# An expert layer that computes every expert, or only each token's two chosen ones

## The reference, cut to what matters

```
flat   = tokens                                  # (2048, 64)
probs  = softmax(flat @ router_w.T)              # 8 experts
p, idx = top_k(probs, 2);  p = p / (sum(p) + 1e-9)
gates  = p scattered to the 8 experts            # (2048, 8), six of the eight are zero
h1 = einsum('nc,ehc->neh', flat, w1)             # e = 8, h = 682
h3 = einsum('nc,ehc->neh', flat, w3)
h  = silu(h1) * h3
y  = einsum('neh,ech->nec', h, w2)               # back to 64 channels
out = einsum('ne,nec->nc', gates, y)
```

## Time and profile before

| | us |
|---|---|
| median of three runs (lowest, highest) | 957.54 (954.67, 958.70) |
| span of the profiled execution, first to last instruction | 952.8 |
| PE busy, PE weight load, DVE, ACT, POOL | 800.3, 594.2, 570.5, 556.2, 366.6 |
| mean granted TensorE clock (1 is full) | 0.741 |

### The profile page before, as it was taken

The page is one execution under the profiler, slowest core; times in us unless marked ns, Lnnn a source line. Parts: engine busy times, 40 slices in busy tenths (PEclk is TensorE's granted clock), DMA queues, the critical chain, the costliest instruction groups (busy, mean ns, idle before and its releaser), DMA issues.

```text
span 952.8 us, 18695 instructions
## 1 busy us (share of the span) xinstructions
PE 800.3 (84%) x6356; PEld 594.2 (62%) x6356; DVE 570.5 (60%) x1752; ACT 556.2 (58%) x1664; POOL 366.6 (38%) x297
## 2 busy tenths in 40 slices
PE   5899987777777776789988768999689999899995
PEld 3587875555655555566666547889446666466663
DVE  3888854556456466334344346887457667467765
ACT  3676752333355365334444355777478888588884
POOL 0878620000000000003000007874268888588884
PEclk7999995555555555555555556999689999899998
DMA  9700000000001100000000000000000100200001
GB/s 224 175 2 1 2 1 1 1 1 1 0 1 78 78 1 1 1 0 1 1 1 1 1 1 1 2 1 2 1 1 2 59 21 2 80 1 2 2 1 23
DMA packets 5860, 18.54 MB, mean 19 GB/s; under 512 B 1093, under 2 KB 2822, under 8 KB 5254
## 3 DMA queue, kind: packets, MB, share of 16 engines
q1 hardware_dynamic: 5478, 17.21, 6.2%
q10 hardware_dynamic: 288, 0.13, 0.1%
HBM read 9.47 MB, written 0.52 MB: 10 GB/s over the span
## 4 chain that ended last, share of the span: by engine, by line
PE 41%; POOL 22%; DVE 13%; issue 11%; ACT 11%; DVEq 1%; POOLq 1%; DMA 0%; SPq 0%; ACTq 0%
POOL zw L1007 21%; PE bank L558 10%; PE bank L383 6%; PE bank L560 6%; PE bank L400 6%; DVE bank L1320 5%; PE bank L348 4%; DVE hr L1324 4%; ACT bank L885 4%; ACT bank L889 4%; PE bank L524 2%; PE bank L370 1%; DVE hid L1089 1%; PE bank L315 1%; PE bank L413 1%
## 5 line engine op out<-in xcount | busy, mean ns | idle before, releaser
L1007 POOL TENSOR_TENSOR zw<-hid,zw 128x512 f16<-128x512 f32 x176 | 203.9, 1159 | 49.3 <-ACT zw L928 38.9
L558 PE MATMUL bank<-hr,lv 64*64 64x8 f32 x512 | 97.0, 261 | 98.8 <-DVE hr L1324 98.4
L966 POOL TENSOR_TENSOR st<-tent,tentx 128x768 f32<-128x768 f32 x72 | 112.2, 1589 | 173.3 <-DVE tentx L1081 123.8
L1443 DVE SCALAR_TENSOR_TENSOR hid<-bank,wsc,st 128x512 f32<-128x512 f32 x176 | 131.9, 750 | 76.0 <-ACT st L932 70.1
L558 PEld LDWEIGHTS bank<-hr,lv 64*64 64x64 f32 x512 | 72.8, 201 | 158.4 <-DVE hr L1324 158.2
L885 ACT ACTIVATE bank<-bank 64x16 f32<-64x16 f32 x256 | 39.2, 153 | 196.8 <-PE bank L560 196.5
L604 PE MATMUL bank<-st,wh 128*128 128x512 f16 x352 | 136.9, 389 | 11.5 <-POOL st L1000 5.4
L932 ACT ACTIVATE st<-bank,wsc 128x512 f32<-128x512 f32 x176 | 120.9, 687 | 39.8 <-PE bank L605 22.0
L605 PE MATMUL bank<-st,wl 128*128 128x512 f16 x352 | 136.8, 389 | 0.0
L966 POOL TENSOR_TENSOR st<-sq 128x768 f32<-128x768 f32 x9 | 13.2, 1498 | 309.3 <-DVE sq L1309 308.5
L1320 DVE TENSOR_TENSOR_SCAN bank<-bank,scan_add 64x24 f32<-64x24 f32 x256 | 52.9, 207 | 127.8 <-ACT bank L885 127.5
(11 more groups left out here) (184 smaller groups left out, 1340.4 us busy)
## 6 DMA issues: line engine op xcount, KB each, us to landing
w13s<-w SPq DMA_DIRECT2D x8, 704.0 KB, 17.9
w2f<-w SPq DMA_DIRECT2D x4, 384.0 KB, 25.4
w13s<-wh SPq DMA_DIRECT2D x2, 704.0 KB, 3.7
w13s<-wl SPq DMA_DIRECT2D x2, 704.0 KB, 5.0
wh<-w13s SPq DMA_DIRECT2D x2, 704.0 KB, 3.9
wl<-w13s SPq DMA_DIRECT2D x2, 704.0 KB, 5.1
w2f<-w2p SPq DMA_DIRECT2D x2, 384.0 KB, 4.9
w2p<-w2f SPq DMA_DIRECT2D x2, 384.0 KB, 5.7
```

What stands on the lines that cost most here:

```text
L558: nc.tensor.matmul(both[:, 0, t, :], lv[:, C:2 * C], prev, start=False, stop=True, skip_group_check=True)
L966: nc.gpsimd.tensor_tensor(st[p][:, t, k:k + KG, :].rearrange("p k (y x) -> p k y x", x=16), ty, tx, ALU.mult)\
L1007: nc.gpsimd.tensor_tensor(hl[:, u % MR, :], hid[:, u % MR, :], hh[:, u % MR, :], ALU.subtract)\
L1443: nc.vector.scalar_tensor_tensor(out=hid[:, u % MR, :], in0=bank[2 + u % 2][:, :], scalar=wsc[:, 5:6], in1=silu[:, u % 2, :], op0=ALU.mult ...
```

## The change

Only the two chosen experts of a token are computed. The 4096 (token, choice) entries are sorted by expert on the chip, each expert's list is padded to whole tiles of 128 entries, and NT = 39 tiles (the most that 4096 entries and 8 experts can need) are always run. The parts:

1. Weights. Each pair's weights lie as two slots of w1 and w3 side by side (2 x 682 columns) instead of padded blocks of 128; 16 pieces a pair are split, in 68 steps of the recurrence, to where they stay. SP's copies are gone; the loads are 52 DMAs instead of 12.
2. POOL makes constants (iotas, a triangle of ones, a float16 identity) between the convolutions.
3. After the logits, PE transposes `xn` to rows of tokens, ACT and POOL split them into high and low float16 parts, and SP writes them to DRAM (`xrows`, 2048 rows of 256 bytes).
4. DVE finds both choices from the logits, counts ranks by a scan, gets totals from two small PE matmuls, and so the place of every entry in the sorted order. 32 one-hot matrices (`lsel`, `tsel`) and 32 PE matmuls invert that order into row numbers (`xidx` for reading, `yidx` for writing), and a table `etab` says which expert a tile has.
5. Per tile: POOL gathers 128 rows of `xrows` (`fetch`, an indirect DMA, four ahead); SP copies that expert's second-layer weights (196 KB) to one of three buffers `w2r` (a register read from `etab` gives the address); PE turns the tokens, runs eight matmuls of 341 columns with the weights as moving operand, turns the hidden values (six float32 transposes) and runs twelve matmuls of 128 columns; ACT, DVE as before but 682 columns wide, and DVE also makes the low part; POOL scatters 128 rows of the result to DRAM (`spread`, an indirect DMA).
6. At the end SP reads the two results of every token back (1 MB), and DVE multiplies by the gates and adds.

There is no hardware loop any more; all 39 tiles are written out. The core of the diff:

```diff
# SP
+            for t in range(NT):
+                e = sp.value_load(etab[0:1, t:t + 1], min_val=0, max_val=E - 1)
+                if t >= 3:
+                    sp.wait_ge(s("m_y"), t - 2)
+                sp.dma_start(w2r[:, t % 3, :], w216[:, bass.ds(e * HP + 2 * HP, HP)])\
+                    .then_inc(s("m_w2" + "abc"[t % 3]), 16)
+            sp.wait_ge(s("m_rows"), 16 * NT)
+            for q in range(2):
+                sp.dma_start(ytok[:, 8 * q:8 * q + 8, :, :] ..., rows[:, q * 1024:q * 1024 + 1024])
# PE
+            for j in range(8):
+                mm = nc.tensor.transpose(bank[4 + j // 4][...], xn[:, j * 128:j * 128 + 128], ident[:, :])
...
+            def turn_tokens(t):
+                pe.wait_ge(s(f"m_g{t % AHEAD}"), 16 * (t // AHEAD + 1))
...
+                nc.tensor.transpose(bank[4][:, 0:64].bitcast(F16), xg[:, t, :], ident16[:, :])
+            def first(t, e):
+                pe.wait_ge(s("m_xts"), t + 1)
+                for m in range(2):
+                    if t > 0:
+                        pe.wait_ge(s(("m_silu", "m_hid")[m]), t)
+                    for half in range(2):
+                        for part in range(2):
+                            mm = nc.tensor.matmul(duo[m][:, half * 512:half * 512 + n], xts[:, t % 3, :],
+                                                  w16[:, bass.ds(e * SLOT + at, n)], ...)      # n = 341
+            def turn_hidden(t):
+                pe.wait_ge(s("m_hid"), t + 1)
+                for b in range(EB):                                                            # EB = 6
+                    mm = nc.tensor.transpose(bank[6 + b // 4][...], htok[:, t % 2, b * 128:...], ident[:, :])
+            def second(t):
+                pe.wait_ge(s("m_w2" + "abc"[t % 3]), 16 * (t // 3 + 1))
...
+                for b in range(EB):
+                    for part in (hh, hl):
+                        mm = nc.tensor.matmul(bank[5][:, 0:2 * C], part[...], w2r[...], ...)
+            for t in range(NT + 2):
+                if t < NT:
+                    first(t, e)
+                    if t + 1 < NT:
+                        e = expert(t + 1)              # value_load on PE
+                        turn_tokens(t + 1)
+                if 1 <= t <= NT:
+                    turn_hidden(t - 1)
+                if t >= 2:
+                    second(t - 2)
# ACT, per tile: gated(t) silu 682 columns; turned_tokens(t + 1) copy of 128; high(t - 1) copies of 512 and 256
# DVE
+            for c in range(32):
+                ins = nc.vector.tensor_scalar(lsel[:, c, :], lane_c[:, :], lane[:, k, g:g + 1], code_v[:, c:c + 1],
+                                              ALU.is_equal, ALU.mult)
...
+            for t in range(NT + 2):
+                if t < NT:
+                    gated(t)                           # 682 columns
+                if 1 <= t <= NT:
+                    low(t - 1)                         # 512 and 256 columns from PSUM
+                if t >= 2:
+                    rows_out(t - 2)                    # reduce_sum 128 -> 64 columns
# POOL
+            for t in range(AHEAD):                     # AHEAD = 4
+                fetch(t)
+            gp.wait_ge(s("m_idx"), 2)
+            for t in range(NT):
+                if t + AHEAD < NT:
+                    fetch(t + AHEAD)                   # waits for turn_tokens(t), then indirect DMA
+                spread(t)                              # waits for rows_out(t), then indirect DMA
```

More of the change, by code:

```diff
@@ new lines, in build @@
+        counts = spare[:, 256:384].rearrange("p (e g) -> p e g", e=E)
+        spots = spare[:, 384:640].rearrange("p (k g e) -> p k g e", k=2, g=16)
+        tiles, ends, start_c = [rk[:, 8 * k:8 * k + 8] for k in range(3)]
+        spot, away, tile_n, lane, gate = [rk[:, 32 * k:32 * k + 32].rearrange("p (k g) -> p k g", k=2)
+                                          for k in range(1, 6)]
+        bits = rk[:, 192:192 + NP40 // 2].bitcast(F16)
+        raw = rk[:, 224:224 + NP40].bitcast(I32)
@@ L287, in _ @@
-            for q in range(2):
[L288 to L296, removed]
+                    mine = w13s[hf * C:hf * C + C, e, :].rearrange("c (k m n) -> c k m n", k=2, m=2)
@@ L590, in _ @@
             mm.then_inc(s("m_log"), 1)
[L591 to L618, removed]
-                            mm = nc.tensor.matmul(bank[4 + 2 * (g % 2) + j // 2][:, lo:lo + n],
-                                                  part[:, u % MR, j * 128:j * 128 + 128], rhs,
-                                                  start=(t == 0 and j % 2 == 0 and part is hh),
-                                                  stop=(t == PT - 1), skip_group_check=True)
-                    if t == PT - 1:
-                        mm.then_inc(s("m_y"), 1)
-                for u in range(U + MLAG):
-                    if u < U:
-                        first(u)
-                    if u >= MLAG:
-                        second(u - MLAG)
@@ new lines, in _, with expert @@
+            pe.wait_ge(s("m_tsel"), 1)
+            for c in range(32):
+                if c % 8 == 0:
+                    pe.wait_ge(s("m_lane"), c // 8 + 1)
+                mm = nc.tensor.matmul(bank[7][:, 64:64 + NP40], lsel[:, c, :], tsel[:, c, :],
+                                      start=(c == 0), stop=(c == 31), skip_group_check=True)
+            mm.then_inc(s("m_code"), 1)
+            def expert(t):
+                return pe.value_load(etab[0:1, t:t + 1], min_val=0, max_val=E - 1)
@@ L903, in _ @@
                     early_tents(image_step(n, 12))
-                for part in range(2):
-                    if SPLIT[part] <= n < SPLIT[part] + 2 * PAIRK:
-                        high_part(2 * PAIRK * part + n - SPLIT[part])
+                if split_piece(n) is not None:
+                    high_part(split_piece(n))
             act.wait_ge(s("l_h"), STEPS + 1)
@@ L1002, in _ @@
[L1002 to L1008 removed]
+            gp.wait_ge(s("c1_sz_done"), NG * B)
+            nc.gpsimd.memset(htok[:, :, HID:HP], 0.0).then_inc(s("m_zero"), 1)
```

542 lines of the change are left out of this document (344 added, 198 removed).

## The result

| | us |
|---|---|
| changed kernel, median of four runs (lowest, highest) | 874.53 (870.66, 878.11) |
| kernel before, four runs | 956.46 (954.67, 958.70) |
| ratio, with its 95% interval | 0.9138 [0.9107, 0.9169] |
| profiled execution of the changed kernel: span, own time | 876.4, 878.11 |

The forecast was 871 us, the range 835 to 920.

A forecast was written before the change was run, and what follows sets the result against it. The prediction took PE's stream of columns to bound the kernel before; its steps summed to a span of 866.3 us, 86.5 less than 952.8, and 957.5 - 86.5 gave 871 us, range 835 to 920 (8 in 10).

The forecast's parts named there:

- Ahead of the logits: Everything before the logits at 684.0 us: weight pieces, POOL's constants and loads add 0, within +-1 us.
- Router: From the logits to the first tile's first matmul: 20.0 us to the indices plus 3.7, at 707.7.
- g: POOL's time to make one indirect DMA: 1.2 us, with ends 0.36 and 2.1.
- L: Time for a gather's DMA to land once made: 1.9 us, up to 2.5.
- The period, 3.6: Tile loop: gathers queued behind scatters on POOL make two periods at least 7.15 us, 3.6 us a tile.
- Start and emptying: Tile loop's ends: 9.6 us to the first `rows_out`, then tile 5's gather at 721.6; pipeline empties in 7.2.
- The end: After the last tile, from 847.6 us: last rows, scatter, 1 MB read-back, products and sums, to 866.3.
- Added waits: PE's `value_load` and SP's ring copy in each tile: 0 us; bounds for the `value_load` 0 to 3.04.
- Rival B: Tile loop bound by PE, POOL's cycle closing in under 2.8 us: about 838 us, chance 0.18.
- C: Tile loop: PE slow through half clock or its sequencer, 4.4 to 4.9 us a tile: 898 to 915, chance 0.23.
- D: Tile loop: POOL walks 128 indices singly and becomes the bound, slower than before from 24 ns an index; chance 0.09.

The follow-up runs named there:

- lag2_load: lag2 with PE's first layer reading constant addresses, `value_load` kept, eight register additions per tile gone, tiles not given their own expert: 833.01 us.
- noring: Changed kernel without SP's copies to the ring; PE reads the second layer's weights in place by a register's address: 870.65 us.
- lag2: Changed kernel with POOL's order alone altered: behind the gather of tile t+4 it scatters tile t-2 in place of t: 840.03 us.
- ahead3: Changed kernel with gathers running three tiles ahead in place of four (`AHEAD = 3`): 1000.03 us.

## Why the prediction was right, point by point

In the profiled span the forecast was 866.3 and the trace has 876.4, 10.1 more. By its steps:

- **Ahead of the logits: 0.** Found +2.7 (686.7 for 684.0). Its own bounds were +-1, so this term was mis-sized. Other profiles of the same code give -1.9 to +3.0, so one profile can't tell this term to +-1. The recurrence starts 4.3 us later than before; what of that is the loads' doing, and how it shrinks again before the logits, stays open.
- **Router, 23.7 to the first tile.** Found 25.2. Within it the 32 `lsel` instructions, for which the bounds were 3.5 and 9.2, took 7.22 for 7.0. The excess is in the hop from `xidx` to POOL (0.88, not counted), the totals on PE (1.19 for 0.9) and two instructions beside POOL:

```profile
688.66 0.29 DVE L1556 TENSOR_REDUCE spare<-xc 128x16 f32<-128x128 f32 x1
688.98 1.13 DVE L1557 TENSOR_TENSOR xc<-xc,spare 128x128 f32<-128x128 f32 x1
690.14 1.12 DVE L1558 TENSOR_TENSOR xc<-xc,rank_c 128x128 f32<-128x128 f32 x1
...
698.46 7.22 DVE L1591 TENSOR_SCALAR st<-lane_c,rk,code_v 128x128 f16<-128x128 f16 x32
```

- **g = 1.2, L = 1.9,** the two unseen prices. Found 1.29 from the start of a scatter to that of the gather behind it, and 0.97 for the making of the gather. Over the gathers of tiles 7 to 38, landing comes 2.74 us after the gather's start at the median and 2.90 at the mean, which leaves 1.8 and 1.9 for L: as forecast. (In the cycle shown above it was 2.4.)
- **The period, 3.6.** Found 3.67 over all tiles, (850.58 - 726.82) / 33 = 3.75 from tile 5 on: +5.0 us in all, the largest part of the miss. The mechanism, its place and its two-period count are shown: one period gives 6.86, three and four give PE's own or nearly. The sum 2.85 + 2.4 + 1.9 = 7.15 is right, and nearly so in its parts: the means over tiles 7 to 38 are 2.68 + 0.28 + 1.29 + 2.90 = 7.15 from a turn to the landing. What it left out is that a turn need not start when its gather lands. It does in 25 of these 32 tiles (0.05 us later); in 7 PE comes to it 0.2 to 4.7 us late, 0.36 at the mean of all 32, hence 7.51 for two tiles. Even and odd tiles are two such cycles that share one PE: a late landing (the gather of tile 7 took 4.83 us) holds up both, and an early one is of no use while PE is still busy with the tile ahead. Twice the granted clock was also down to half for about one tile's work, in and behind a long wait: 4.96 us from the turn of tile 7 to that of 8 and 4.27 from 26 to 27, where PE's own is 2.56 (windows of the changed kernel, columns as above):

```profile
735.00:741.90 6.90, 5.97 (x33) 4.84 (x34) 2.02 (x4) 2.22 (x5) 1.95 (x2) 0.51 0.12 38
806.70:810.10 3.40, 3.40 (x22) 2.83 (x22) 1.32 (x3) 1.12 (x3) 0.29 (x1) 0.50 0.05 10
742.00:806.60 64.60, 48.77 (x484) 37.85 (x483) 38.65 (x73) 34.53 (x71) 35.19 (x36) 1.00 0.24 75
```

  Tiles 5 to 9 and 26 to 27, in which these two stretches lie, hold 2.7 + 0.7 of the 5.0 us; the other 28 tiles, at full clock, hold 1.6.
- **Start and emptying.** From the first matmul to the turn of tile 5, 14.9 for 13.9; from the last turn to the start of the last sum 8.3 for 7.2.
- **The end, 18.7.** Found 17.5 from the start of the last sum (858.9). The read-back of 1 MB, worked out from the earlier trace rows as 5.2 us, took 5.4 from its issue at 861.6 to here:

```profile
867.02 1.23 DVE L1654 TENSOR_TENSOR st<-st,rk 128x1024 f32<-128x1024 f32 x1 [7.86 <-DMA st<-yrows]
```

- The rest is in the times. 2.7 + 1.5 + 1.0 + 5.0 + 1.1 - 1.2 = 10.1 in the span; this execution is 3.6 above its median, and a run's time is 1.7 to 1.9 above its span here, where the forecast had set 4.7 between the profiled span and the median of before. 10.1 - 3.6 - 3.0 = 3.5, which is 874.5 against 871. So the final number agrees better than the steps do, and that part is luck, from the scatter between executions; the steps were good to 1.2% of the span. (In them, 0.426 ns for each of 128 columns is 0.055 us, not 0.056: 0.02 us a tile.)
- **Added waits: 0.** Right for the `value_load` in the changed kernel, and lag2_load shows that it stays right without slack where the additions are gone. The step did not name the additions to registers as a cost in itself. In the changed kernel PE is idle 0.9 us a tile, and six more additions in noring did not make it slower; in lag2 leaving out the eight wins 0.15 a tile.
- **Rival B** (PE-bound, 838 us) is what lag2 is: 840.0, and the period of 2.56 that the forecast took from columns is that of the kernels without additions, 2.57. **C** did not set the period: of PE's idle time ahead of the turns 36.0 us went to gathers and 0.5 to "issue". Its half clock came about in the two short stretches above, and in ahead3, where PE idles more, for most of the time (0.70 at the mean). **D:** POOL's price per index is 0.9 ns, not 24.
- The Trainium skill's rule behind D (GPSIMD Engine Reference, Performance pitfalls for Q7 kernels), by which 128 indices would take 10.9 us, an estimate from that page, does not hold for this instruction: 0.97 us. The Trainium skill's other page (DMA: Bandwidth & Descriptors, Anatomy of one DMA) gives 2.1 us for the whole, again an estimate, and is nearer: 2.7 us at the median from issue to landing. The floor of 0.6 us for `tensor_load` in the Trainium skill (DMA: Bandwidth & Descriptors, Latency and other measured facts) is above the traces' row of 0.30; with the 0.15 behind it, 0.45.

## What to carry to other kernels

When one in-order engine issues both the loads of later tiles and the stores of earlier ones, write down the cycle through it (result, store, next load, landing, result) and divide by the number of tiles between its ends: where that quotient is longer than any engine's busy time per tile, it is the floor of the period. The measured period lies above it when the landings scatter, since the cycles share engines that work in order. Here two more turns between a tile's sum and its scatter, a change of three lines, won 34.5 us (lag2 beats both kernels, 840.0 us, 0.8778 [0.8755, 0.8801] of before). And judge a side edit only with the bound it will meet: leaving out the ring copies gave 3.9 us less under one bound (not clear of noise) and 10.1 more under the next.

## What the runs showed of the hardware that was not expected

- Making an indirect DMA on POOL takes 0.97 us for 128 rows of 256 bytes and 0.91 for 64; the next starts 0.30 us later.
- Address additions (FUSED_REGOPS, 46 ns each) in PE's program cost time once PE is the bound: six more on top of eight made a tile 0.27 us longer, all of their 0.28; leaving out the eight won 0.15 of their 0.37. A register load on the same queue (0.30 us) cost nothing once the additions were gone.
- The gathers' landings scatter (2.4 to 4.8 us from issue, median 2.7), and in the changed kernel the granted clock fell to half in one long wait of PE for a gather (3.8 us, up to 735.9) and just behind another (2.5 us, up to 806.4), while a third (2.5 us, up to 777.4) went by at full clock.
